# A graph network's dense steps in a new order, with x1's four tiles shared by three engines

## The reference

```
e      = x[src] * (1 + softplus(c) * edge_weight)
pooled = relu(layer_norm(e @ pool_w + pool_b) * g_p + b_p)
agg    = segment_max(pooled, dst), at least 0
h      = relu(layer_norm([x, agg] @ final_w + final_b) * g_f + b_f)
x1     = norm(x + h)
a[i,b] = mean over the edges into i of comp[type, b] * x1[src]     (8 bases)
out    = norm(x1 + [a, x1] @ weight + bias)
```

## Time and profile before

| | |
|---|---|
| runs | 882.5 us median of 3 (880.93 to 883.58) |
| the profiled execution | 882.3 us, span 880.5 us |
| TensorE, VectorE, ScalarE, GpSimd busy | 90%, 88%, 68%, 80% of the span |
| mean granted TensorE clock | 0.957 |
| ramp of the dense stage | to about 58 us |
| steady dense steps | 58.6 to 474.6 us |
| edge groups | to about 626 us |
| last stage | to the end |

### The profile page before, as it was taken

How to read it: one execution, slowest core, us unless ns; L and a number is a source line. 1 busy time by engine, 2 the same in 40 slices (tenths; PEclk the granted TensorE clock), 3 DMA queues, 4 the chain that set the end, 5 groups by cost and what they waited for, 6 DMA issues and landing times.

```text
span 880.5 us, 17875 instructions
## 1 busy us (share of the span) xinstructions
PE 793.3 (90%) x4519; PEld 553.4 (63%) x4519; DVE 775.1 (88%) x2703; ACT 601.5 (68%) x2887; POOL 703.4 (80%) x703
## 2 busy tenths in 40 slices
PE   4699999999999999999999999997499998989760
PEld 3577777777777777777777787775345544434340
DVE  6999999999999999999999999986179999999780
ACT  4699999999999999999999988885202121111130
POOL 2599899899899899899898577776677777777777
PEclk9899999999999999999999999999589999999895
DMA  4366676666666666676666534444187887878711
GB/s 115 107 221 221 214 241 219 214 219 221 210 219 222 209 221 218 207 222 221 211 219 199 172 123 124 134 149 144 48 291 280 321 285 287 303 271 303 270 47 46
DMA packets 90699, 179.84 MB, mean 204 GB/s; under 512 B 17161, under 2 KB 36018, under 8 KB 84326
## 3 DMA queue, kind: packets, MB, share of 16 engines
q1 hardware_dynamic: 73414, 147.26, 50.1%
q0 software_dynamic: 15744, 30.96, 11.2%
q10 hardware_dynamic: 1440, 0.50, 0.3%
HBM read 109.02 MB, written 70.91 MB: 204 GB/s over the span
## 4 chain that ended last, share of the span: by engine, by line
PE 56%; POOL 23%; issue 9%; DVE 6%; ACT 3%; DMA 3%; ACTq 0%; POOLq 0%; DVEq 0%
PE ps L586 13%; PE ps L554 13%; POOL out_rows L431 11%; POOL rows L438 11%; PE ps L565 6%; PE ps L539 5%; PE ps L611 4%; PE ps L578 4%; PE ps L548 4%; PE ps L600 3%; PE ps L610 2%; POOL x_table L486 2%; PE ps L589 2%; DMA x_table<-agg_all,scat_x 1%; ACT junk L767 1%
## 5 line engine op out<-in xcount | busy, mean ns | idle before, releaser
L767 ACT ACTIVATE junk<-ps 128x128 bf16<-128x128 f32 x884 | 233.0, 287 | 21.1 <-PE ps L589 12.3
L767 ACT ACTIVATION_READ_ACCUMULATOR junk<-ps 128x1 f32 x884 | 193.6, 219 | 0.0
L719 PE MATMUL ps<-agg_all,w_cen 128*128 128x512 f32 (+1 forms) x400 | 178.0, 599 | 3.1 <-DVE agg_all L1271 2.5
L431 POOL DMA_INDIRECT x_dst<-in_x,dst_i x98 | 153.5, 1566 | 14.9 <-issue 4.5
L586 PE MATMUL ps<-w_cen,xT 128*128 128x128 f32 x984 | 157.8, 292 | 1.4 <-ACT xT L827 1.4
L461 POOL TENSOR_TENSOR work<-work,vec_raw 128x512 f32<-128x512 f32 x98 | 124.6, 1272 | 35.4 <-DVE work L1171 24.7
L586 PEld LDWEIGHTS ps<-w_cen,xT 128*128 128x128 f32 x984 | 127.9, 195 | 30.2 <-issue 27.9
L554 PE MATMUL ps<-w_cen,work 128*128 128x128 f32 x984 | 146.2, 293 | 0.0
L1271 DVE TENSOR_TENSOR agg_all<-coefs,ps 128x1024 f32<-128x1024 f32 x98 | 117.7, 1210 | 29.7 <-PE ps L705 18.3
L554 PEld LDWEIGHTS ps<-w_cen,work 128*128 128x128 f32 x984 | 122.3, 196 | 28.8 <-issue 28.8
L1107 DVE BATCH_NORM_STATS2 bn<-work 128x6 f32<-128x128 f32 x492 | 133.0, 276 | 0.7
(11 more groups left out here) (147 smaller groups left out, 1399.8 us busy)
## 6 DMA issues: line engine op xcount, KB each, us to landing
coefs<-coef_line SPq DMA_DIRECT2D x49, 1024.0 KB, 7.4
rows<-in_x SPq DMA_DIRECT2D x97, 256.0 KB
x_table<-work SPq DMA_DIRECT2D x97, 256.0 KB, 2.1
out_rows<-outb SPq DMA_DIRECT2D x97, 256.0 KB, 2.1
x_dst_table<-x_dst SPq DMA_DIRECT2D x98, 64.0 KB
rows<-x_dst_table SPq DMA_DIRECT2D x24, 256.0 KB
apart<-apart_line SPq DMA_DIRECT2D x14, 224.0 KB
x_dst<-in_x,dst_i POOLq DMA_INDIRECT x98, 4.0
```

The costliest lines, as they stand in the source:

```text
L431: return pool.indirect_dma_start(*args, bounds_check=last_node, oob_is_err=False)
L719: last = pe.matmul(MT[b][:, 0:n * D], w_cen[:, W_BASE + m, :], prod[:, b, m, 0:n, :].rearrange("p t d -> p (t d)"), start=(m == 0), stop=( ...
L767: last = nc.scalar.activation(junk[:, kind * CH + m, :], bank[:, cols(m, m + 1)], ACT.Square, accum_out=power[:, b, 1, TOP + kind * CH + m ...
```

## The change: what it does

- In dense groups x1's four tiles are made by ACT (tiles 0 and 1), DVE (tile 2) and POOL (tile 3, `fourth_x1`, a 128x128 tensor_tensor, at the end of POOL's list of the step). SP's store, PE's `turned` and ACT's `roots` wait for POOL's tile as well. In edge groups ACT makes two and DVE two.
- DVE: the residual comes after the spread; `pooled_scaled` comes ahead of `first_layer`.
- ACT: `first_layer` comes ahead of `rooted` in dense steps. PE: `first_bias` comes ahead of `rooted` in dense steps.
- PE's `first_bias` no longer waits for scatters to land.

```diff
--- before.py
+++ after.py
@@ -214,7 +214,7 @@
         names = ("first_in", "pool_in", "rest_in", "coeff_in", "e_weight_in", "vectors_in", "bases_in", "rows_of_dst_in", "index_in", "edges_in", "mask_made", "mask_stored",
                  "types_in", "comp_in", "types_cast", "types_t", "onehot_made", "onehot_pe", "onehot_copied", "line_pe", "line_made", "const_ready", "ident_ready", "scat_ready",
                  "setup_dve", "bases_dve", "base_sums", "bases_ready", "soft_dve", "soft_act", "pe_a", "act_a", "pe_b", "pe_e", "act_h", "dve_q", "act_q", 
-                 "dve_t", "dve_te", "pool_b", "apart_stored", "agg_ready", "act_e", "scaled", "e_ready", "dve_v", "dve_x", "act_x", "dve_o", "pe_c", "pe_cp", "act_c", "dve_scan", "pe_d",
+                 "dve_t", "dve_te", "pool_b", "apart_stored", "agg_ready", "act_e", "scaled", "e_ready", "dve_v", "dve_x", "pool_x", "act_x", "dve_o", "pe_c", "pe_cp", "act_c", "dve_scan", "pe_d",
                  "act_y", "act_o", "dve_own", "deg_dve", "deg_pe", "root_centred", "col_sums", "root_ready", "c_own", "pe_g", "act_g",
                  "dve_prod", "pe_m", "dve_y", "dve_sum", "pe_s", "dve_r", "act_r", "act_out")
         S = {n: sem(n) for n in names}
@@ -237,7 +237,7 @@
         W_TOP, W_POOL, W_BOT, W_ROOT, W_BASE = 0, 1, 2, 3, 4
         GAM_F, BET_F, GAM_P, BET_P = 3, 4, 5, 6
         N_CONST = 10
-        X1_ACT = CH - 1
+        X1_ACT = CH - 2
 
         def tiles_in(q):
 
@@ -376,6 +376,7 @@
                 if is_dense(c, 4):
                     sp.wait_ge(S["act_x"], s - 3)
                     sp.wait_ge(S["dve_x"], s - 3)
+                    sp.wait_ge(S["pool_x"], s - 3)
                     b_ = x1[:, b, :, :].rearrange("p c d -> p (c d)")
                     tail = c - 4 == DENSE - 1
                     sp.dma_start(x1_tail if tail else x1_groups[s - 4], b_[0:TAIL] if tail else b_) \
@@ -450,6 +451,17 @@
                 pool.wait_ge(src_in[slot], 16 * (t // SLOTS + 1))
                 r = rows[:, slot, SRC, :]
                 pool.tensor_tensor(r, r, e_scale[:, t:t + 1].broadcast_to([P, D]), ALU.mult).then_inc(S["scaled"], 1)
+
+            def fourth_x1(s):
+                c, b = s, s % 2
+                if is_dense(c, 4):
+                    pool.wait_ge(S["act_q"], s - 1)
+                    need(pool, S["pe_c"], s - 5)
+                    if is_dense(c, 6):
+                        pool.wait_ge(x1_stored[b], 16 * since(c, 4 + b, 2))
+                    pool.tensor_tensor(x1_tile(c - 4, CH - 1), hn[:, (c - 4) % SLOTS, CH - 1, :],
+                                       st[:, 7, TOP - 1:TOP].broadcast_to([P, D]), ALU.mult) \
+                        .then_inc(S["pool_x"], 1)
 
             def step(s):
                 b = s % 2
@@ -472,6 +484,7 @@
                 if is_tile(s, -3):
                     need(pool, S["pe_a"], s)
                     gather_src(s + 3 - LATE)
+                fourth_x1(s)
                 if is_group(s, 4) and not is_dense(s, 4):
 
                     d = s - 4 - DENSE
@@ -534,6 +547,8 @@
                     if is_group(c, 5):
                         pe.wait_ge(S["act_x"], s - 4)
                         pe.wait_ge(S["dve_x"], s - 4)
+                        if is_dense(c, 5):
+                            pe.wait_ge(S["pool_x"], s - 4)
                         need(pe, S["act_c"], s - 5)
                         for m in range(CH):
                             last = pe.transpose(VT[:, cols(m, m + 1)], x1_tile(c - 5, m), ident[:, :])
@@ -569,9 +584,6 @@
                     if c == 1:
                         pe.wait_ge(S["setup_dve"], 1)
                     if is_group(c, 1):
-                        d = c - 1 - DENSE - LEAD
-                        if d >= 0:
-                            pe.wait_ge(x1_scattered[d % LEAD], 16 * CH * (d // LEAD + 1))
                         need(pe, S["dve_t"], s - 2)
                         if is_group(c, 3) and not is_dense(c, 3):
                             pe.wait_ge(S["dve_v"], s - 2)
@@ -614,8 +626,8 @@
                 if c < EDGE_ORDER:
                     turned()
                     root_bias()
+                    first_bias()
                     rooted()
-                    first_bias()
                     first_layer()
                     rows_turned()
                     pooled_turned()
@@ -777,6 +789,8 @@
                 def roots():
                     if 2 <= c <= GROUPS + 3:
                         act.wait_ge(S["dve_q"], s - 1)
+                        if is_dense(c, 5):
+                            act.wait_ge(S["pool_x"], s - 4)
                         if is_group(c, 5):
                             act.wait_ge(S["act_x"], s - 4)
                         nc.scalar.activation(st[:, 7, :], st[:, 6, :], ACT.Sqrt, scale=float(D)).then_inc(S["act_q"], 1)
@@ -841,8 +855,8 @@
                 if c < EDGE_ORDER:
                     turned()
                     roots()
+                    first_layer()
                     rooted()
-                    first_layer()
                     squares()
                     pooled_squares()
                     rows_turned()
@@ -1120,10 +1134,10 @@
                                                  rows[:, (c - 3) % SLOTS, 0:CH, :].rearrange("p c d -> p (c d)"),
                                                  ALU.max, ALU.add).then_inc(S["dve_v"], 1)
 
-                residual()
                 if stats:
                     own.need(first)
                     spread_at = spread(RES, TOP)
+                residual()
 
                 def variances():
                     if not stats:
@@ -1198,10 +1212,10 @@
                             dve.wait_ge(S["pe_b"], s - 3)
                         if is_dense(c, 4) and is_dense(c, 6):
                             dve.wait_ge(x1_stored[b], 16 * since(c, 4 + b, 2))
-                        for m in range(X1_ACT, CH):
+                        for m in range(X1_ACT, CH - 1 if is_dense(c, 4) else CH):
                             last = dve.tensor_scalar(x1_tile(c - 4, m), hn[:, (c - 4) % SLOTS, m, :],
                                                      st[:, 7, RES + m:RES + m + 1], None, ALU.mult)
-                            if m < CH - 1:
+                            if m < (CH - 2 if is_dense(c, 4) else CH - 1):
                                 own.mark(last)
                         last.then_inc(S["dve_x"], 1)
 
@@ -1219,9 +1233,9 @@
                     stats_of(1)
                     roots_ready()
                     scaled()
+                    pooled_scaled()
                     first_layer()
                     stats_of(2)
-                    pooled_scaled()
                     stats_of(3)
                     dense_out()
                     edge_beta_added()
```

## The result

| | before | after |
|---|---|---|
| median of 3 runs | 882.5 us | 959.5 us (958.43 to 960.82) |
| ratio to before | | 1.088, 95% interval 1.084 to 1.091 |
| profiled execution, span | 882.3, 880.5 us | 959.5, 957.4 us |
| dense step (mean of 85 steps, start to start of POOL's beta addition) | 4.73 us | 5.60 us |
| first scatter starts | 495.0 us | 573.4 us |

The account below looks back on a forecast made before the run. It took a ring of DVE and POOL, joined by semaphores and holds, to bound the dense step: 882.3 + 79 (dense stage) + 5 (ramp) + 1 (end) - 5 (edge groups) = 962 us, range 900 to 985.

Parts of the forecast that it names:

- What bounds the kernel, and what joins DVE and POOL: Dense step, 4.73 us: a ring of DVE and POOL; SBUF-to-SBUF DVE work stands still under POOL tensor operations begun first.
- The tile falls into the beta addition, 0.98 a step: Dense step: DVE's x1 tile starts 0.09 behind L461 and is held, 0.98 us by L938; by L431 only 0.26.
- DVE without collisions, 4.50: Dense step: moving the residual behind the spread saves 0.23 us, so DVE's own loop falls from 4.73 to 4.50.
- The second hold, 0.15: Dense step: the spread L1090 is held by POOL's L452, adding 0.15 us; bounds 0 and 0.33.
- The rule of the Trainium skill: DVE and GpSimd share a port pair; whoever issues first blocks the other for its whole instruction.
- Rival 2: Dense step: L1090 held to L452's end, 0.33; step 5.81 us, 978 us, to 990 if L1095 is held too; 8%.
- POOL's sum, hidden: Dense step: POOL's work with the fourth tile is 4.65 us, or 5.23 with a long L431, hidden in 5.63.
- Dense stage, 88 x 0.90 = 79, ramp 5, end 1: Dense stage: 88 steps growing from 4.73 to 5.63 us cost 79 us, eight ramp steps 5, the last ones 1.
- Edge groups, -5: Edge stage: without the brake the scatters' wait goes, -5 us (-7.5 to 0); wrong if scatters take over 126 us.
- A sign that came out otherwise: Whole kernel: TensorE, DVE and ACT were all to be less busy for the same work.
- The clock stays at 1.00: TensorE, dense stage: clock stays at 1.00, as earlier when busy 1.82 of 3.40 us; here it is over 75%.

Follow-up runs that it names:

- experiment 6: Changed kernel, but DVE makes no x1 tile in dense groups (three on ACT, one on POOL): 864.3 us, ratio 0.977.
- experiment 3: Changed kernel, but POOL's beta addition also waits for DVE's x1 tile of the step before: 897.7 us, ratio 1.015.
- Experiment 1: Changed kernel with DVE's x1 tile put back ahead of pooled_scaled: 860.5 us, ratio 0.974.
- experiment 2: Kernel before with only pooled_scaled moved ahead of DVE's x1 tile: 966.8 us, ratio 1.093.
- experiment 8: Edge-group runs: Experiment 1's kernel with three tiles on ACT, one on DVE (0.972), or with the brake (first_bias's scatter wait) back (0.981); kernel before without brake (0.9955).
- experiment 7: Kernel of Experiment 1 with the residual put back ahead of the spread: 899.2 us, ratio 1.017.
- Experiment 4: Changed kernel with POOL's x1 tile given back to ACT (three on ACT, one on DVE in dense groups): 956.3 us, ratio 1.082.

## Why the prediction was right

962 was forecast and 959.5 measured. The step is right, 5.60 for 5.63, by the mechanism named. That the total comes so near is in part luck: the steady steps gave 77 for 79, ramp and end about 1 for 6, the edge groups -1.5 for -5, and the last two errors nearly cancel. By its steps:

- *What bounds the kernel, and what joins DVE and POOL.* Right. The margin by which L461 leads was given as 0.09 and is 0.09 to 0.10. One reading was too wide: not every DVE operation from SBUF to SBUF is held (experiment 6). Another doesn't hold in general: in experiment 3 the gather isn't long though the residual starts beside it (last section).
- *The tile falls into the beta addition, 0.98 a step.* Right, by experiments 1, 2, 3 and 6. Measured from L1216's start to the next start: 1.18, against 0.19: 0.99. The value from L938 was the one to take, and that from L431 (0.26) was not the earlier trace rows.
- *DVE without collisions, 4.50.* Close: from L1098 to the first statistics are 1.30 with a hold in it, in place of 1.19 + 0.15. But L1104 follows L1098 after 0.18, not 0.29.
- *The second hold, 0.15.* Place wrong, size nearly right. L1104 came 0.05 before L453 and went free; the residual behind it, 0.03 after L453, lasts 0.94 in place of 0.69. The hold is 0.25. With the 0.11 from the point above the two nearly cancel: step 5.60, forecast 5.63. Experiment 1, without collisions, has 1.16 from L1098 to the first statistics, so 0.14 of the 0.25 goes on the path, and 4.47 + 0.99 + 0.14 = 5.60.
- *The rule of the Trainium skill.* "SBUF — State Buffer", section "Who interferes with whom", has the second of the two blocked for the whole instruction. For DVE's one-source tile the trace agrees to 0.01 us. For the two-input residual behind L453 the hold ends about 0.3 us after L453's start (356.13 + 0.25 = 356.38, L453 to 356.51), so again a little before its end. Rival 2, worked out by that rule, came out 18 us too long (978 against 959.5); what it held, L1104, went ahead of L453 and was not held at all.
- *POOL's sum, hidden.* Right; idle time 0.85 a step in place of 0.5 to 0.7, because the gaps around the new tile are 0. The hold of L439 behind the residual, allowed for with 0.3, is there: 1.26 in place of 0.98.
- *Dense stage, 88 x 0.90 = 79, ramp 5, end 1.* The steady part is right (88 x 0.875 = 77); the whole stage up to the first scatter grew by 78.4, so ramp and end cost about 1 together. In the ramp few tiles are held: of the seven made before 58 us five last 0.28, and the addition that came at 56.3 comes at 57.0. What paces the ramp was not tested.
- *Edge groups, -5.* The step that failed. It counted on all of the 3.6 us gap and more. Measured -1.5, and the scatters take 128.8 us, over the 126 that was named as the sign of its being wrong. The gap is gone: behind the first scatter no wait is over 1.5 us. But shorter waits have come at other groups. Of the 11.6 us for DVE's tiles 4.3 lie ahead of the first scatter, where the kernel before waited 4.4 for ACT's tiles; behind it they are 7.3, where they were 8.5. The brake alone is worth 4.0 us by its time and 2.4 by the scatters (experiment 8); what takes back the rest here is not shown.
- *A sign that came out otherwise.* DVE was to be less busy, as TensorE and ACT are. It is busier, 871 us in place of 775, since its busy time holds the time in which the tile stands still.
- *The clock stays at 1.00.* Wrong, and without a price. The row that it rested on, 1.00 with TensorE busy for 1.82 of 3.40 us, didn't carry over: it is 0.91 in the dense stage with TensorE busy for 266 of 300 us (busy time by stretch, columns as in the earlier trace rows: after, then the kernel of experiment 2):

```profile
100.00:400.00 300.00, 265.98 (x1665) 206.40 (x1664) 298.88 (x965) 234.65 (x1241) 234.90 (x269) 0.91 0.59 185
```

```profile
100.00:400.00 300.00, 261.55 (x1647) 189.01 (x1647) 292.27 (x955) 237.17 (x1273) 220.06 (x213) 1.00 0.59 183
```

The clock falls to its lower level (1.2 GHz) in short stretches. The steps are as long with it as without: a mean of 5.59 us for the 32 steady steps that have over 1 us of it, and 5.59 for the 37 that have none. TensorE isn't the limit there.

## What to carry to other kernels

When an operation of VectorE that can be held (here a tensor_scalar from SBUF to SBUF, or one with two SBUF inputs) and a tensor operation of GpSimd become ready at the same signal, find out which starts first: a tenth of a microsecond decides here between 0.27 and 1.26 us, in 91 of 98 steps. Behind such a signal put the operation that can be held first, and the one that reads PSUM after it. And a change of many edits that would be a gain (2.6% faster) can come out as a loss (8.8% slower) by one line of it: where the trace names the line, move that one alone.

## What was not expected of the hardware

- GpSimd's work is drawn out too, its DMA-issuing work included. The edge scaling (L452 there) took 0.87 for 0.41 in experiment 2, 0.06 behind the residual; L439 takes 1.26 for 0.98 in the changed kernel, 0.54 behind it; the gather L432 takes 1.49 for 1.04 in experiment 7, 0.12 behind it.
- When the two start together, the recorded starts don't tell which is held. In the kernel before, over 78 steady steps, the gather L431 starts from 0.013 ahead of the residual to 0.007 behind it and always lasts 1.59 to 1.60. In experiment 3 it (L432) starts 0.002 to 0.017 behind it and always lasts 1.04 to 1.05, with the residual at 0.74 in place of 0.69:

```profile
353.14 0.74 DVE L1134 SCALAR_TENSOR_TENSOR work<-work,rows 128x512 f32<-128x512 f32 x1
353.15 1.05 POOL L432 DMA_INDIRECT x_dst<-in_x,dst_i  x1 [0.15 <-issue]
```

  Experiment 6 is like experiment 3. What the long gathers share is DVE's order (the residual ahead of the spread); why that decides was not tested.
- Even an instruction on four numbers a row is held: 0.53 us for 0.15 (experiment 3).
- The granted clock was 0.91 in the changed kernel and 1.00 in that of experiment 2, with as much TensorE work in steps that are even longer. TensorE's longest pause between 100 and 400 us is 0.41 us in the first and 0.45 in the second. Experiment 4 has 0.91 too; experiment 3, with the same orders on TensorE and ACT and steps of 4.90, has 1.00. What makes the difference was not tested.
- On one chip the same program (the kernel before without the brake) took 51 us longer over its scatters and 43 longer in the last stage, while the dense steps were the same to 0.01 us. ACT's long idle times there are put down to no instruction of this core; the cause is open.
